# Two macaron feed-forward layers around an attention layer: attention scores in another number format, with the maxima in wider pieces and one ring of PSUM banks

## The reference

```python
xd = (x @ W_down).reshape(b, t, h, s)            # b=8, t=1024, h=16 heads, s=16
keys = einsum('bthk,hik->bthi', xd, tokeys) * scale      # scale = 16 ** -0.25
queries = einsum('bthk,hik->bthi', xd, toqueries) * scale
values = einsum('bthk,hik->bthi', xd, tovalues)
dot = einsum('bqhs,bkhs->bhqk', queries, keys)
attn = softmax(dot, axis=-1)
out = einsum('bhqk,bkhs->bqhs', attn, values).reshape(b, t, e)
return out @ W_unify + b_unify
```

## Time and profile before

| | us |
|---|---|
| median of 3 runs | 3145.11 |
| profiled execution | 3149.36 |
| its span | 3147.6 |
| TensorE busy | 2916.1 |
| VectorE busy | 2240.3 |
| ScalarE busy | 1850.9 |
| POOL busy | 745.7 |
| L1486, 2048 reductions of 512 columns | 1297.1 |
| L1466, 2048 exponentials of 512 columns | 1099.6 |
| L1322 and L1331, 4096 score matmuls | 802.0 and 779.9 |
| L1340, 4096 records of the value product | 553.2 |

### The profile page before, as it was taken

The page is one execution under the profiler, slowest core; times in us unless marked ns, Lnnn a source line. Parts: engine busy times, 40 slices in busy tenths (PEclk is TensorE's granted clock), DMA queues, the critical chain, the costliest instruction groups (busy, mean ns, idle before and its releaser), DMA issues. The chain is left out here.

```text
span 3147.6 us, 57549 instructions
## 1 busy us (share of the span) xinstructions
PE 2916.1 (93%) x17263; PEld 1661.5 (53%) x17263; DVE 2240.3 (71%) x4484; ACT 1850.9 (59%) x3505; POOL 745.7 (24%) x759
## 2 busy tenths in 40 slices
PE   5999998859999999999999999999999859999987
PEld 3899998722333333333333333333333248999987
DVE  6655457548888887878887888888888376555565
ACT  5444456514666665766765666666666654444564
POOL 3353125440200300300200201101100034531353
PEclk8999999968999999999999999999999979999988
DMA  5211124231131231222212222231311052111242
GB/s 172 61 40 54 40 73 133 82 91 37 36 81 48 61 76 30 69 67 48 75 42 49 75 49 41 75 68 27 88 35 35 14 162 61 48 45 47 80 131 70
DMA packets 185826, 206.09 MB, mean 65 GB/s; under 512 B 29496, under 2 KB 149248, under 8 KB 185600
## 3 DMA queue, kind: packets, MB, share of 16 engines
q1 hardware_dynamic: 177408, 192.74, 22.7%
q0 software_dynamic: 8192, 10.57, 1.1%
HBM read 146.79 MB, written 55.66 MB: 64 GB/s over the span
## 5 line engine op out<-in xcount | busy, mean ns | idle before, releaser
L1486 DVE TENSOR_REDUCE at_mxc<-at_pb 128x1 f32<-128x512 f32 x2048 | 1297.1, 684 | 303.4 <-PE at_pb L1322 283.5
L1466 ACT ACTIVATE at_ex<-at_pd 128x512 f32<-128x512 f32 x2048 | 1099.6, 597 | 557.5 <-PE at_pd L1331 557.1
L1322 PE MATMUL at_pb<-at_ka,at_qa 96*128 96x512 bf16 x2048 | 802.0, 392 | 40.8 <-DMA at_qa<-at_scr 18.2
L1331 PE MATMUL at_pd<-at_qa,at_ka 99*128 99x512 bf16 x2048 | 779.9, 383 | 25.0 <-DMA at_qa<-at_mparts 19.7
L768 DVE TENSOR_TENSOR f_ml_hl<-f_ml_h,f_ml_hh 128x512 fp32r<-128x512 f32 (+1 forms) x384 | 288.1, 752 | 425.6 <-ACT f_ml_hh L844 424.6
L1322 PEld LDWEIGHTS at_pb<-at_ka,at_qa 96*128 96x128 bf16 x2048 | 200.2, 98 | 695.4 <-DVE at_mxc L1486 496.0
L1340 PE MATMUL at_po<-at_ex,at_va 128*32 128x512 f32 x4096 | 553.2, 610 | 9.6 <-DVE at_os L1574 5.6
L841 ACT ACTIVATE f_ml_h<-f_ml_pL,b1T 128x512 f32<-128x512 f32 (+1 forms) x384 | 244.1, 636 | 451.9 <-PE f_ml_pL L895 448.5
L910 PE MATMUL f_ml_pA<-f_wh,f_ml_hh 128*128 128x256 f32 (+1 forms) x1408 | 409.6, 291 | 0.0
L912 PE MATMUL f_ml_pA<-f_wl,f_ml_hh 128*128 128x256 f32 (+1 forms) x1408 | 402.1, 286 | 0.0
L913 PE MATMUL f_ml_pA<-f_wh,f_ml_hl 128*128 128x256 f32 (+1 forms) x1408 | 402.0, 286 | 0.0
(11 more groups left out here) (143 smaller groups left out, 2981.2 us busy)
## 6 DMA issues: line engine op xcount, KB each, us to landing
f_wraw<-in_L_ffn_w SPq DMA_DIRECT2D x128, 256.0 KB, 2.8
at_scr<-at_parts SPq DMA_DIRECT2D x96, 256.0 KB
at_ka<-at_scr SPq DMA_DIRECT2D x64, 256.0 KB, 5.2
at_qa<-at_scr SPq DMA_DIRECT2D x64, 192.0 KB, 3.9
f_ro_xr<-in_L_attn_x SPq DMA_DIRECT2D x16, 512.0 KB, 3.9
f_ml_xr<-in_L_attn_x SPq DMA_DIRECT2D x16, 512.0 KB, 4.2
x<-f_ml_yo SPq DMA_DIRECT2D x16, 512.0 KB, 4.0
at_xr<-x SPq DMA_DIRECT2D x16, 512.0 KB, 4.7
```

The costliest lines, as they stand in the source:

```text
L1322: eng.matmul(pb[place(c)][:, :], qa[g][0:KROWS, qh, j, qt * P:(qt + 1) * P], ka[g][0:KROWS, j, kh * 512:(kh + 1) * 512], start=True, stop= ...
L1331: eng.matmul(pd[place(c)][:, :], ka[g][0:KROWS + MROWS, j, kt * P:(kt + 1) * P], qa[g][0:KROWS + MROWS, qh, j, :], start=True, stop=True). ...
L1466: eng.activation(ex[t % 2][:, j, :], pd[place(GH * t + j)][:, :], ACT.Exp).then_inc(s_ex.sem, 1)
L1486: eng.tensor_reduce(mxc[:, c % CH:c % CH + 1], pb[place(c)][:, :], AX.X, ALU.max).then_inc(s_mx.sem, 1)
```

## The change

Queries and keys are cut into two float32r parts instead of three bf16 parts (a float32r matmul multiplies numbers of a shortened mantissa that are stored in four bytes). Three products of parts lie on 3 x 16 = 48 rows, with two rows for the maximum 50, so two heads fit on the array's two row halves (partitions 0 to 63 and 64 to 127, `HALF`). `qa` and `ka` hold heads j with e = j % 2 as the half and p = j // 2 as the place. In a step the matmuls alternate between the halves: the maxima's products take e = 0, 0, 1, 1 (two per 1024 columns of one buffer), the exponentials' products heads ORDER = 1, 3, 0, 2, that is e = 1, 1, 0, 0.

The maxima are reduced over all 1024 keys at once: pb is two buffers of two banks each, and a step has two reductions instead of four; the second reduction that joined halves of 512 and negated is gone, and the sign is applied when `mx` is read.

PSUM holds pb (four banks), po (one) and three banks pd, which form one ring (`Ring`) for both the exponentials' tiles and the side products: tile n of the ring uses bank n % 3 and waits until tile n - 3 has been read out. px is gone. Each side product also waits until the one before it has been read. VectorE reads a side product of step t - 1 after the first of the two reductions of step t. `times_v` stands after the third pair of score matmuls, in steps 0 and 8 after the fourth. The copy of po moves from VectorE to ScalarE, between its third and fourth exponential. POOL no longer splits; it writes eight memsets of ones (the upper rows of each half of `ka`) before its first rstd. The parts are float32r in `scr` (two planes of four bytes instead of three of two), stored right after the last `qk`; a unit has 12 load DMAs and the maxima four instead of three.

```diff
-Q_PARTS = [0, 1, 2, 0, 1, 0]
-K_PARTS = [0, 0, 0, 1, 1, 2]
+Q_SLOTS = [0, 0, 1]
+K_SLOTS = [0, 1, 0]
+HALF = P // 2
+RING = 3
...
-        pb = [ps(f"pb{i}", [P, 512]) for i in range(BANKS)]
-        pd = [ps(f"pd{i}", [P, 512]) for i in range(BANKS)]
+        pb = [ps(f"pb{i}", [P, T]) for i in range(2)]
+        pd = [ps(f"pd{i}", [P, 512]) for i in range(RING)]
         po = ps("po", [P, 512])
-        px = ps("px", [P, 512])
...
+class Ring:
+    def full(self, n):
+        return n + 1 + self.per * self.i
+    def before(self, n):
+        return n // RING + self.per // RING * self.i
+    def freed(self, n):
+        return n // RING + 1 + self.per // RING * self.i
...
+            def for_max(b, g, t, e, kh):
+                qh, p, qt = t // NT, t % NT // 4, t % 4
...
+                if kh == 0:
+                    eng.wait_ge(s_mx.sem, s_mx.at(2 * (ST * unit(b, g) + t) + e - 1))
+                rows = slice(HALF * e, HALF * e + KROWS)
+                mm = eng.matmul(pb[e][:, kh * NQ:(kh + 1) * NQ], qa[g][rows, qh, p, qt * P:(qt + 1) * P],
+                                ka[g][rows, p, kh * NQ:(kh + 1) * NQ], start=True, stop=True)
...
+            def for_exp(ring, b, g, t, j, n):
+                qh, kt, e, p = t // NT, t % NT, j % 2, j // 2
...
+                eng.wait_ge(s_free[n % RING].sem, s_free[n % RING].at(ring.before(n)))
...
+            def side_product(ring, a):
+                bank = pd[a.n % RING]
+                eng.wait_ge(s_free[a.n % RING].sem, s_free[a.n % RING].at(ring.before(a.n)))
+                if a.after is not None:
+                    eng.wait_ge(s_free[a.after % RING].sem, s_free[a.after % RING].at(ring.freed(a.after)))
...
                     for i in range(4):
                         if ahead:
-                            scores_for_max(b1, g1, 4 * t + i)
-                        if not ends:
-                            scores(*((b, g, t + 1) if t < ST - 1 else (b1, g1, 0)), i)
-                        if i == 1:
-                            times_v(b, par, g, t)
-                    if now:
-                        aux(now)
+                            for_max(b1, g1, t, i // 2, i % 2)
+                        if tiles:
+                            for_exp(self.ring, *coming, ORDER[i], tiles[i])
+                        if i == (3 if starts else 2):
+                            times_v(self.ring, b, par, g, t, done)
+                    if a:
+                        side_product(self.ring, a)
...
+            def maximum(b, g, t, e):
+                r = 2 * (ST * unit(b, g) + t) + e
+                eng.wait_ge(s_b.sem, s_b.at(r + 1))
+                col = 8 * e + t % NT
+                eng.tensor_reduce(mxc[:, t // NT, col:col + 1], pb[e][:, :], AX.X, ALU.max).then_inc(s_mx.sem, 1)
...
+                    for e in range(2):
                         if ahead:
-                            maxima(b1, g1, 4 * t + i)
-                        if i == 1:
-                            aux(before)
+                            maximum(b1, g1, t, e)
+                        if e == 0 and self.late:
+                            side_out(self.ring, self.late)
+                    self.late = a
```

More of the change, by code:

```diff
@@ L1205, in phase @@
                 for t in range(ST):
-                    task = task_at(g, t, prev, last)
-                    now, n, ns = None, self.n, self.ns
+                    done = self.ready[-1]
+                    ends = last and g == 3
+                    b1, g1 = next_unit(b, g)
+                    coming = (b, g, t + 1) if t < ST - 1 else (b1, g1, 0)
+                    tiles = None
+                    if not (ends and t == ST - 1):
+                        tiles = self.ready = [self.ring.take() for _ in range(GH)]
@@ L1218, in phase @@
-                    do.step(b, par, g, t, n, ns, before, now, last)
-                    before = now
-        def place(c):
-            return 1 if c == ST * GH - 1 else c % BANKS
-        def back(c):
-            return next(d for d in range(1, ST * GH) if place((c - d) % (ST * GH)) == place(c))
-        unit = lambda b, g: 4 * b + g
-        next_unit = lambda b, g: (b, g + 1) if g < 3 else (b + 1, 0)
+                        a = self.place(task, b, par, g)
+                    do.step(b, par, g, t, coming, tiles, done, a, side, not ends, last)
```

471 lines of the change are left out of this document (234 added, 237 removed).

## The result

The changed kernel takes 3991.8 us (median of 4 runs, 3977.6 to 4008.8) against 3150.0: a ratio of 1.268, 95% interval 1.261 to 1.274. That is 27% slower; 3400 was predicted, 3640 was the range's upper end. The profiled execution has a span of 3983.4 us, 835.8 more than before.

The account below looks back on a forecast made before the run. TensorE was taken as the bound before the change, waits in the queues after it. The profiled 3149.4 us + 238 (attention steps) + 15 (before them) = 3402, stated as 3400 us; range 3200 to 3640.

Parts of the forecast that it names:

- Rival A: Attention stage: TensorE's clock sags to 1.2 GHz a fifth (3530 us) or two fifths (3680) of the time; chance 0.22.
- step (3): PSUM ring of three banks: i = 2 score tile waits for VectorE to evacuate a side product; `qk` step 4.75 us.
- step (5): Before the first attention step: memsets delay the rstd, side products wait for one another, the store grows; sum +15 us.
- Step (1): Attention scores: two f32r matmuls on different row halves take 0.23 us for both, 0.46 if one after the other.
- Step (2): Maxima in two buffers of 1024 columns: one reduction takes 1.21 us, the refill loop makes a plain step 3.02 us.
- The deduction for the first unit and the last batch, -42: Attention steps: the first unit has no output products and the last batch prepares none; -42 us.
- The -5 for POOL's split: Before the first step: the low split on POOL behind the last `qk` goes; -5 us.
- Steps (4) and (6): Attention steps: the os copy moved to ScalarE costs nothing; DMA taken as 0, with ends of -20 and +20 us.
- B: Attention stage: halves do not overlap, the ring's wait is milder; step 3.4 to 3.7 us, 3130 to 3290; chance 0.08.
- C: Attention stage: E2's slot is free in time in all steps, plain loop 3.02 us; total 3088 us; chance 0.10.
- E2: The exponentials' i = 2 tile in the ring, said to wait until the preceding step's side product is evacuated.

Follow-up runs that it names:

- e3: The changed kernel with VectorE reading the side product ahead of its first reduction and the value product always after the fourth score pair; 3177.3 us, 1.0075.
- e10: e9 with the side product kept behind the value product where t % 8 = 7; 3084.8 us, 0.976.
- e8: e5 with each score matmul taking the rows of both halves (112 and 114 for 48 and 50), spare rows zeroed; 3671.0 us, 1.164.
- e5: The changed kernel with ORDER (0, 2, 1, 3), so both score matmuls of a pair use the same row half; 4668.9 us, 1.482.
- e4: The changed kernel with the i = 2 maxima product issued three times more in steps behind `qk`, `mx`, `f` and `u`; 3920.4 us, 1.244.
- e2: The changed kernel with the value product always behind the fourth pair of score matmuls; 3708.7 us, 1.177.
- e7: e3 with the side product ahead of the value product and POOL's memsets moved behind its two `rstd`; 3166.6 us, 1.0042.
- e12: The changed kernel with SP's list alone split as in e9, other engines' orders kept; 3972.5 us, 1.258.
- e9: e7 with SP storing the first half at an earlier `qk` and waiting for a landing only ahead of the load needing it; 3106.3 us, 0.983.

## Why the prediction was wrong

The direction and the main mechanism were right: the order of the queues turned TensorE from the bound into a waiter (e3 gives 815 of 842 us back by order alone). The time was wrong by 592 us. By its steps:

**Rival A, the clock: the step that failed most.** The forecast's chance of 0.60 rested on a stage at full clock, because before the change a drop followed a full stop and not gaps below 2 us. The changed kernel has gaps of 1.1 to 1.9 us (the four lines above, each divided by its count) in 28 steps of 64, as forecast, and is at 1.2 GHz for half of its stage, where A had a fifth to two fifths. A's length of a low step was about right (5.5 for 3.9, 1.41 times; the 91 steps wholly at 1.2 GHz take 1.47 times their full-clock medians), its share of time was too small, and the range ended at 3640, below A's own case of two fifths. (Its sums are slightly off too: they give 2124 and about 3520 and 3660 us, not 2130, 3530 and 3680.) The clock is 385 us of the 592; 184 are step (3)'s and the two before it, 11 step (5)'s, the other 12 lie behind the last step and between the profiled execution and the median. The weighing compared gaps with gaps in the earlier trace rows, and took the stage before as granted 1.00 where that row has 0.98; it left out that the change cuts the scores from 96 and 99 rows to 48 and 50. The runs show a part for both. With the gaps mostly gone the half-row pairs keep 0.99 (e10), so rows alone do not bring the low clock; with the gaps kept and 112 and 114 rows fed it is 4% of the time (e8) against 83% (e5), so gaps alone do not either. Why the clock falls is not shown beyond this: e8 changes operands and position on the array with the rows, and e4 filled only half of the gaps. The rule that stood beside A, the Trainium skill's (TensorE: Matmul & The Clock Gate, section A second HAM failure mode: psum-queue depth-cycling), names micro-idles between groups of matmuls alone. This case's trace agrees that the clock swings between its two levels, with a mean of 0.72 to 0.74 in the stage; e8, with the micro-idles kept and 0.98 granted, shows that here they were not enough for it.

**Step (3), `qk`: the loop runs through TensorE.** Predicted 4.75 us, measured 5.55. I followed VectorE's queue (second reduction + 1.13, then the next step's first). The timeline has that reduction idle 0.49 us ahead of 1872.26: its halves stand on TensorE behind the `qk` product. By that way: 1.43 to the i = 3 pair (1870.02), 0.42 to the `qk` product, 1.05 to the next step's first pair (1871.49), 0.34 to the second, 0.43 to the reduction, 1.14, and 0.74 through the side operation to the next: 5.55. The prediction had left the side product's own time out of the `qk` loop, and had it in that of `u`. `mx` (4.34, measured 4.55), `f` (4.53, 4.91), `xd` (4.13, 4.53) and `v` (3.5, 3.76) were 5 to 9% short, `u` (5.81, 6.42) 10%.

**Step (1), the pair.** Two halves do start together (1870.02 and 1870.02), so that bound was the right one. The next pair comes after 0.34 us (1871.49 to 1871.83) where a value product or a side product stands ahead of the first one, and after 0.24 otherwise (1871.83 to 1872.07; the median of the full-clock cases is 0.34 and 0.24 in this trace and in e10's). So 0.23 was right for the pairs but the first. Why the first costs 0.10 more is not shown. The weight load, 0.18 to 0.19 us where the bf16 scores' took 0.10, is not enough to explain it, since the float32r matmuls of the earlier trace rows have one as long and start 0.23 us apart:

```profile
100.16 0.19 PEld L894 LDWEIGHTS f_ml_pL<-f_ml_xTl,f_wh 128*128 128x128 f32 x1
```

From a score matmul to the value product it is 0.43, not 0.33.

**Step (2), the plain step.** 3.02 predicted, 3.24 measured: 0.43 + 1.00 + 0.52 + 1.22 + 0.07. Of the difference 0.10 is the way to the value product and 0.09 the way from the maxima's last half to its reduction. The reduction of 1024 columns was right: 1222 ns for 1.21 us, repeating after 1.14 for 1.13. e2 confirms the loop itself. (The deduction for the first unit and the last batch, -42, adds up to -40 from its own terms.)

**Step (5), before the steps.** +15 predicted, +26.1 measured. The memsets and their effect on POOL were right (timeline of POOL in the changed kernel):

```profile
640.58 14.79 POOL L1641 MEMSET at_ka<- 32x2048 f32 x8
655.45 1.04 POOL L165 TENSOR_TENSOR at_ln_rstd<-at_ln_ve,neghalf 128x4 f32<-128x4 f32 x1
```

Eight take 14.8 us for 15, the first `rstd` is 12.4 us later for 9.5 (3.1 of them because the stage itself starts later). e7 won only 3 us because the memsets it moved then slow VectorE down. From there the starts in the two timelines give the rest: first `rstd` to first `qk` product 23.4 us for 16.6 (side products one after another, +7, where +9 was priced), first `qk` product to the first store 12.2 for 11.9, the store to the first load 14.7 for 11.2 (+3.5 for an allowance of 3), the load to the first score matmul 11.5 for 10.3, and the maxima 39.3 for 38.6 where -2 was priced. The -5 for POOL's split is nowhere to be seen.

**Steps (4) and (6).** The copy on ScalarE costs nothing that shows; ScalarE idles 1149 us before its exponentials. DMA at 0 was about right for the changed kernel (e12 wins under 1%) and would have been wrong by 60 us in a faster one (e9).

**Rivals B and C.** B did not come: the halves overlap, and the ring's waits were longer than forecast, not milder. C said that E2's slot is free in time; it was not, until the orders were mended. The prediction's objection to it, the queues, was what decided. That C's 3088 is close to e10's 3085 is luck: C had plain steps of 3.02 us, 52 of them, and the old stops; e10 has plain steps of 2.61 and longer ones behind the side products (2.96 to 4.60), and SP's list mended as well.

## What to carry to other kernels

When buffers are merged or made scarcer, write for each engine the order in which it takes and frees them, and follow the loop through every queue, the producer's own other work included. Here two places in two queues made 26%; with the side products' place on TensorE and SP's list changed as well, a kernel slower by 27% became one faster by 2.4%, of which 1% was to be had in the kernel before by SP's list alone. When TensorE stops being the bound, price its clock as a term of its own, and look at the array rows that its matmuls feed as well as at its gaps: in this kernel the matmuls of half the rows kept the full clock only where they ran side by side with few waits. And when a piece of work is moved off a path, look at what runs beside it in its new place.

## What the runs showed that was not expected

- Float32r matmuls of 50 rows, one after the other on a half, had a granted clock of 0.58 between 1500 and 2000 us; with 114 rows behind nearly the same waits it was 0.98 (the operands' numbers and the place on the array differ too).
- At full clock, pairs of float32r matmuls on two row halves repeat after 0.24 us, hardly more than the 0.23 of single full-height ones, but after 0.34 for the first pair behind a value product or a side product.
- Filling about half of the waits with more half-row matmuls lowered the time at 1.2 GHz only from 50% to 42%.
- Eight memsets of 14.8 us ahead of a layer norm's `rstd` held it up by 9 us; moved behind it they ran beside four VectorE operations, which took 7.64 us in place of 1.38.
